# The expert block of a decoder layer: 14 whole tiles of 128 tokens in seven groups of two, instead of 16 batches of 112 tokens in four groups of four

## The chip, the core and the metric

The kernel runs on one core of a Trainium2 chip, in float32 for the part that matters here. The metric is the device time of one execution in microseconds (us). Matrix products run on TensorE (PE in the profile; PEld are its weight loads), the rest on VectorE (DVE), ScalarE (ACT) and GpSimd (POOL); SyncE (SP) issues all transfers.

## What is computed

A decoder of six sublayers over x of 16 batches x 112 tokens x 256 channels: causal linear attention, cross attention, an "ffn" block that holds a causal attention of its own and four experts, latent attention, windowed cross attention with rotary positions, and a ternary linear layer. The change touches the experts:

```python
xf = _rms(x, n2_w).reshape(-1, C)            # 1792 tokens x 256
logits = jnp.nan_to_num(xf @ gate_w.T)       # 1792 x 4
probs = jax.nn.softmax(logits, axis=-1)
topv, topi = jax.lax.top_k(probs, K)         # K = 2 of 4 experts
topv = topv / (topv.sum(-1, keepdims=True) + 1e-08)
wts = zeros(N, 4).at[arange(N)[:, None], topi].add(topv)
o0 = _gelu(xf @ e0_up.T) @ e0_down.T
o1 = jax.nn.silu(xf @ e1_w1.T) * (xf @ e1_w2.T) @ e1_down.T
o2 = _gelu(_gelu(_gelu(xf @ e2_l1.T) @ e2_l2.T) @ e2_l3.T) @ e2_l4.T
o3 = _gelu(_gelu(xf @ e3_down.T) @ e3_up.T) @ e3_out.T
moe = wts[:, 0:1] * o0 + wts[:, 1:2] * o1 + wts[:, 2:3] * o2 + wts[:, 3:4] * o3
moe = moe.reshape(B, T, C).at[:, :, :64].set(0.0)
return x + moe
```

All four experts are computed for every token; the weights `wts` choose afterwards. Hidden widths are 512 (256 for the first product of expert 3).

## The kernel before

Every engine has a program of its own, written out by hand, and the engines are tied by semaphores; there is no planner. Each engine executes its program in order. Nearly all matrix products go through one helper (`products`, whose line is L272), and nearly all transposes of rows through another (`transposes`, L265), so those two lines stand for many places of the code.

Tokens lie in rows: X holds 112 partitions (the tokens of a batch) x 16 x 256. The expert block has three parts.

**Preparation** (`phase_g`). For each of the 16 batches DVE scales 112 rows by their RMS factor (L1793), PE turns them into columns (L265), and ACT copies these into `m_xfT`, 128 channels x 2 x 1792 tokens, with the norm weight as scale (L1380). Four batches are prepared ahead of the first product; the other twelve are interleaved with the first twelve "up" products (`beside`).

**Gate.** Four products of gate weights (128x4) with 448 tokens each give logits as four rows of a bank; ACT copies them (L1395), 16 small transposes (L965) bring them back to tokens in rows, and DVE computes softmax, top 2 and weights in a chain of dependent steps (`weights`, L1810 to L1832), with one exponential on ACT (L1401).

**Experts** (`phase_m`). Four groups of `QUAD` = 4 batches, so `QN` = 448 token columns. The first group is written out, the other three are a loop. In a group PE makes 30 "up" products, each of 128 outputs x 448 tokens, contracted over 256 or 512 channels, so 2 or 4 matmuls of `QN` columns; in all 76 matmuls. In the profile each float32 matmul is two PE instructions, so 152. They rotate over four banks: product n may start when ACT has read product n-4. ACT reads them with GELU, Tanh or Copy (L1413 to L1419); DVE multiplies gate and up parts of expert 1 (L1842, L1845). The "down" products have tokens in rows as output: for each expert and batch a 112x192 result over 512 hidden channels (4 matmuls with 112 weight columns and 192 moving columns), 64 matmuls or 128 PE instructions in a group. DVE multiplies each with the token's weight and adds it to X (L1856).

After the last group all engines wait for the last of these additions (`M["acc"]`), and the latent attention starts on X, batch by batch, with layer norm statistics on DVE (L1764).

SP's queue is one program as well: in the causal attention before the experts it issues one small transfer of row maxima in each step (`maxima`, L470) and one expert weight after it (L371).

Of the kernel before, what the change touches and what calls it, by code (L numbers as in the profile page):

```python
# [28 lines left out]
ALU = mybir.AluOpType  # L29
# [26 lines left out]
UPS = 30  # L56

# [81 lines left out]
def decoder_kernel(nc, T, out):  # L139
    ctx = ExitStack()  # L140
    with ctx:
# [12 lines left out]
        X = sb("X", [S, B * D])  # L154
# [16 lines left out]
        def xb_(b, lo=0, hi=D):  # L171
            return X[:, bass.ds(b * D + lo, hi - lo)]

# [13 lines left out]
        gate = sb("gate", [P, KT, 4])  # L187
# [158 lines left out]
        m_xfT = take(P, KT * B * S, "p (k n) -> p k n", k=KT)  # L346
        g_xf = [take(S, D) for _ in range(2)]
        g_lt = take(4, B * S)
        g_lg = take(S, B * 4)
        g_a, g_b2, g_w = take(S, B * 4), take(S, B * 4), take(S, B * 4)  # L350
        g_red, g_red2 = take(S, B), take(S, B)
        g_cmp, g_cmp2 = take(S, B * 16), take(S, B * 16)
        m_g, m_s, m_u, m_t = (take(P, 2 * QN, "p (g n) -> p g n", g=2) for _ in range(4))
        m_h0, m_h1, m_ha, m_hb = (room[:, i * FT * QN:(i + 1) * FT * QN].rearrange("p (k n) -> p k n", k=FT) for i in range(4))
        m_hc = room[:, 4 * FT * QN:4 * FT * QN + KT * QN].rearrange("p (k n) -> p k n", k=KT)
        m_hd = take(P, FT * QN, "p (k n) -> p k n", k=FT)
# [20 lines left out]
        def _(sp):  # L377
            x_rows, x_out = T["x"].rearrange("b s d -> s b d"), X[:, :].rearrange("s (b d) -> s b d", b=B)
# [38 lines left out]
            wload(sp, gate[:, :, :], "gate", ld["gate"])  # L417
# [63 lines left out]
            sp.wait_ge(pre["pad"].sem, 3)  # L481
# [39 lines left out]
        def _(pe):  # L521
# [427 lines left out]
            def phase_g(b, u, half):  # L949
                pe.wait_ge(G["xf"].sem, G["xf"].at(b + 1))  # L950
                pe.wait_ge(G["xte"].sem, G["xte"].at(b - 1))
                transposes(g_xf[u], S, KT, pb[4 + u]).then_inc(G["xt"].sem, 1)

            def gate_of(i):
                pe.wait_ge(G["xte"].sem, G["xte"].at(QUAD * (i + 1)))
                if i > 1:
                    pe.wait_ge(G["ls"].sem, G["ls"].at(i - 1))
                products(pb[6 + i % 2][0:4, 0:QN], [gate[:, k, :] for k in range(KT)],
                         [m_xfT[:, k, i * QN:(i + 1) * QN] for k in range(KT)]).then_inc(G["lt"].sem, 1)

            def logits():
                pe.wait_ge(G["ls"].sem, G["ls"].at(B // QUAD))
                pe.wait_ge(G["xte"].sem, G["xte"].at(B))
                for b in range(B):
                    last = T3.transpose(pb[4][0:S, 4 * b:4 * b + 4], g_lt[:, b * S:(b + 1) * S], ident[0:4, 0:4])  # L965
# [14 lines left out]
            for b in range(QUAD):  # L980
                phase_g(b, b % 2, 0)


            def phase_m(i, first):
                use = [0]

                def up(w, m, src, kn, ready):
# [7 lines left out]
                    products(pb[n % 4][:, 0:QN], [w[:, k, m * P:(m + 1) * P] for k in range(kn)],  # L995
# [4 lines left out]
                def xf(k):  # L1000
                    return m_xfT[:, k, bass.ds(i * QN, QN)]
# [1002 lines left out]
```

## Time and profile before

| | |
|---|---|
| median of 3 runs | 1403.35 us (1402.88 to 1403.44) |
| profiled execution, its own time | 1402.48 us |
| span of its instructions | 1400.4 us |
| PE busy | 1333.6 us (95% of the span) |
| DVE, ACT, POOL busy | 738.0, 499.6, 286.4 us |
| mean granted TensorE clock | 0.987 of full speed |
| expert block, first up product to last addition | 750.07 to 1075.6 us |

Busy time of PE counts a matmul from its start to its modelled end; successive matmuls overlap in it. So the time that one matmul takes of a stream is read here as the distance from one start to the next: the start of one row of the timeline minus the start of the row before, divided by the instructions of the earlier row. Within one row, the last instruction starts at the row's end less the duration of one. An instruction's form is written as weight rows*weight columns, output shape, or as output<-input; `128*112 128x192` is a matmul with 112 weight columns and 192 moving columns.

### The profile page before, as it was taken

How to read it: one execution, taken by the hardware profiler on the slowest of the kernel's cores; microseconds unless marked ns; L12 is line 12 of the kernel's file. 1: busy time of each engine (PE TensorE's matmuls, PEld its weight loads, DVE VectorE, ACT ScalarE, POOL GpSimd, SP SyncE). 2: the span in 40 equal slices, each digit the busy share in tenths (PEclk: the TensorE clock that was granted, in tenths of full speed). 3: DMA queues.
4: the chain of work that ended last, by engine and by line, in shares of the span. 5: the costliest groups of instructions: out<-in, count | busy, mean ns of one | idle time of the engine just before them, and what ended most of it. 6: DMA issues, size and time to landing. Idle time of an engine off the chain costs nothing.

```text
span 1400.4 us, 30973 instructions
## 1 busy us (share of the span) xinstructions
PE 1333.6 (95%) x12381; PEld 922.9 (66%) x12381; DVE 738.0 (53%) x1715; ACT 499.6 (36%) x972; POOL 286.4 (20%) x380
## 2 busy tenths in 40 slices
PE   6999999988999999899988999999999899999996
PEld 5777888754666665467664575665757676777764
DVE  5666666654666664477743122020112555678886
ACT  2111111102555555356645223121221444444444
POOL 2000000102211221688724000000001100224431
PEclk9999999997999999999999999999999999999999
DMA  7212211102222220012200200000000000000001
GB/s 208 60 42 54 43 31 31 30 24 52 61 48 66 53 54 7 1 59 67 70 12 1 56 1 1 0 0 0 0 0 1 3 4 3 13 17 16 16 6 54
DMA packets 46995, 44.34 MB, mean 32 GB/s; under 512 B 14512, under 2 KB 43552, under 8 KB 46864
## 3 DMA queue, kind: packets, MB, share of 16 engines
q1 hardware_dynamic: 46864, 42.49, 11.9%
q8 instruction: 95, 1.56, 0.5%
q14 instruction: 36, 0.29, 0.1%
HBM read 38.95 MB, written 2.78 MB: 30 GB/s over the span
## 4 chain that ended last, share of the span: by engine, by line
PE 87%; ACT 4%; issue 3%; DVE 3%; POOL 2%; DMA 0%; ACTq 0%; DVEq 0%; POOLq 0%
PE banks L272 48%; PE banks L736 7%; PE banks L715 4%; PE banks L911 3%; PE banks L853 3%; PE banks L866 3%; PE banks L906 3%; PE banks L265 2%; PE banks L847 2%; PE banks L583 2%; PE banks L752 2%; ACT area L1280 2%; PE banks L541 2%; PE banks L894 2%; ACT area L1357 1%
## 5 line engine op out<-in xcount | busy, mean ns | idle before, releaser
L1620 DVE TENSOR_REDUCE Y_room<-banks 112x2 f32<-112x750 f32 x128 | 115.4, 936 | 85.9 <-PE banks L715 85.9
L1716 DVE TENSOR_REDUCE area<-banks 112x8 f32<-112x896 f32 x96 | 100.2, 1086 | 77.1 <-PE banks L853 77.1
L1280 ACT ACTIVATE area<-banks,Y_room 125x896 f32<-125x896 f32 x96 | 96.7, 1007 | 97.0 <-PE banks L736 87.1
L1357 ACT ACTIVATE area<-banks 112x896 f32<-112x896 f32 x96 | 82.8, 914 | 121.1 <-PE banks L911 121.1
L272 PE MATMUL banks<-room,area 128*112 128x256 f32 (+1 forms) x384 | 120.7, 465 | 3.8 <-issue 3.4
L1856 DVE SCALAR_TENSOR_TENSOR X<-banks,area,X 112x192 f32 (+1 forms) x64 | 26.5, 417 | 160.0 <-PE banks L272 160.0
L736 PE MATMUL banks<-room,area 64*125 64x224 f32 x768 | 100.0, 379 | 6.9 <-ACT area L1280 5.7
L272 PE MATMUL banks<-area,room 128*128 128x224 f32 x512 | 103.5, 362 | 2.0 <-ACT area L1233 2.0
L1413 ACT ACTIVATE room<-banks 128x448 f32<-128x448 f32 x72 | 39.2, 544 | 181.8 <-PE banks L272 181.8
L272 PEld LDWEIGHTS banks<-area,room 128*128 128x128 f32 x512 | 97.8, 194 | 4.6 <-ACT area L1233 2.3
L272 PE MATMUL banks<-room,l 128*128 128x448 f32 x256 | 97.9, 540 | 0.0
L251 POOL TENSOR_TENSOR rstd<-mv,kcol 112x1 f32<-112x1 f32 x32 | 6.1, 192 | 437.4 <-DVE mv L1455 437.4
L272 PEld LDWEIGHTS banks<-room,area 128*112 128x112 f32 x384 | 67.9, 182 | 41.1 <-issue 27.8
L736 PEld LDWEIGHTS banks<-room,area 64*125 64x125 f32 x768 | 65.7, 186 | 33.6 <-ACT area L1280 23.1
L1151 POOL TENSOR_TENSOR area<-area,kcol 112x32 f32<-112x32 f32 x16 | 87.2, 5451 | 1.3
L1222 ACT ACTIVATE area<-area,minus_one 128x448 f32<-128x448 f32 x64 | 42.8, 668 | 115.8 <-DVE area L1498 115.8
L265 PE MATMUL banks<-cst,area 112*128 112x112 f32 x416 | 65.5, 269 | 19.0 <-DVE area L260 10.7
L265 PEld LDWEIGHTS banks<-cst,area 112*128 112x128 f32 x416 | 46.8, 143 | 51.8 <-issue 45.1
L272 PEld LDWEIGHTS banks<-room,l 128*128 128x128 f32 x256 | 48.5, 190 | 47.6 <-issue 47.6
L1181 POOL MEMSET area<- 112x16 f32 x1 | 0.1, 125 | 318.5 <-DVE X L1856 318.5
L272 PEld LDWEIGHTS banks<-dn,room 128*112 128x112 f32 x384 | 62.6, 177 | 3.1 <-issue 3.1
L1498 DVE TENSOR_TENSOR area<-banks,bqk 128x448 f32<-128x448 f32 x64 | 39.9, 623 | 46.9 <-PE banks L272 39.8
(233 smaller groups left out, 2473.7 us busy)
## 6 DMA issues: line engine op xcount, KB each, us to landing
area<-den_scratch SPq DMA_DIRECT2D x32, 224.0 KB, 3.8
Y_room<-in_ctx SPq DMA_DIRECT2D x16, 375.0 KB
area<-in_ctxT SPq DMA_DIRECT2D x64, 93.8 KB
l<-in_l SPq DMA_DIRECT2D x2, 1024.0 KB, 5.2
room<-in_ctxT SPq DMA_DIRECT2D x16, 112.0 KB, 2.2
out<-X SPq DMA_DIRECT2D x16, 112.0 KB, 1.9
X<-in_x SPq DMA_DIRECT2D x1, 1568.0 KB, 21.9
room<-in_Wq SPq DMA_DIRECT2D x1, 1024.0 KB, 6.1
```

The lines of the kernel that those rows point to most:

```text
L265: last = nc.tensor.transpose(dst[:, k * parts:(k + 1) * parts], src[:, k * P:(k + 1) * P], ident[0:parts, 0:parts])
L272: last = nc.tensor.matmul(dst, a, w, start=(k == 0), stop=(k == len(lhs) - 1))
L715: last = T3.matmul(pb[r][0:S, 0:SC], b_q[w][o:o + HD + 2, k, r % 2, :], b_ctx[w][o:o + HD + 2, k, 0:SC], start=True, stop=True)
L736: last = T3.matmul(pb[4 + e][0:KC, 2 * i * S:2 * (i + 1) * S], b_ctx[w][o:o + 2 * SLOT, k, c * KC:(c + 1) * KC], b_q[w][o:o + 2 * SLOT, k, ...
L853: last = T3.matmul(pb[2 + j][0:S, c:c + S], c_qd[g % 3][o:o + SLOT, k, e, :], c_kT[g % 3][o:o + SLOT, k, :], start=False, stop=(k == 1 and ...
L866: last = T3.matmul(pb[6][SLOT * a:SLOT * a + HD + 1, t * S:(t + 1) * S], c_v[n % 2][:, 4 * t + a, :], c_pT[:, c:c + S], start=True, stop=True,
L1151: g_.tensor_tensor(c_r[n % 2], c_r[n % 2], kcol[:, 0, :], ALU.pow).then_inc(W["r"].sem, 1)
L1222: a_.activation(a_e[:, g % 2, :], a_z[:, g % 2, :], ACT.Exp, bias=minus_one[:, :]).then_inc(A["ex"].sem, 1)
L1280: a_.activation(b_pT[g][:, c, :, :], banks[0:KC, 4:6, 0:QN], ACT.Exp, bias=b_bias[v][:, c:c + 1]).then_inc(Bs["ex"].sem, 1)
L1357: a_.activation(c_pT[:, i * 8 * S:(i + 1) * 8 * S].rearrange("p (j n) -> p j n", j=2), banks[0:S, 2 + 2 * i:4 + 2 * i, 0:4 * S], ACT.Exp). ...
L1620: v_.tensor_reduce(b_nb[u][:, 4 * a + k:4 * a + k + H + 1:H], banks[0:S, 2 * a:2 * a + 2, 0:SC], AX_X, ALU.max, negate=True).then_inc(Bs[" ...
L1716: v_.tensor_reduce(c_nb[:, 8 * i:8 * i + 8].rearrange("q (j n) -> q j n", j=2), banks[0:S, 2 + 2 * i:4 + 2 * i, 0:4 * S].rearrange("q j (n ...
```

## The change

- X gets 128 partitions. The tokens of batches 0 to 13 stay where they are, in rows 0 to 111 of 14 tiles. Those of the last two batches are cut into seven pieces of 16 tokens each, and piece j fills rows 112 to 127 of tile j (batch 14) or 7+j (batch 15). 14 x 128 = 1792, so no row is empty.
- For the columns this is only a matter of where ACT writes: the columns of batch 14 and 15 go to seven places of 16 columns each. Batch 14 is prepared first (`XF_ORDER`), three batches ahead of the first product instead of four.
- `phase_m` takes two tiles (256 columns) at a time in seven groups; six of them are the loop.
- Down products have 128 weight columns (tokens) instead of 112; there are 2 per expert and group.
- The gate's weights are padded to 32 columns, and four blocks of up to 512 tokens are multiplied on four column groups of PE, in one bank; 4 transposes of up to 128x128 replace the 16 small ones. The weight chain on DVE runs on 128 partitions x 14 tiles instead of 112 x 16.
- Rows 112 to 127 of X collect only expert output: SP sets them to zero with 14 small transfers ahead of the first `maxima`. After group 3 seven transfers of 16 rows x 192 bring the pieces of batch 14 back into a 112-row tile beside the weights, after the last group seven more bring batch 15, issued in step 4 of the latent attention; DVE adds each of the two tiles to X before the statistics of batches 14 and 15.

```diff
+WHOLE = B - 2
+PIECE = P - S
+TILES = WHOLE
+PER = 2
+GN = PER * P
+GROUPS = TILES // PER
+ACCS = 4 * PER
+XF_ORDER = [WHOLE] + list(range(WHOLE // 2)) + [WHOLE + 1] + list(range(WHOLE // 2, WHOLE))
...
-        X = sb("X", [S, B * D])
+        X = sb("X", [P, B * D])
-        gate = sb("gate", [P, KT, 4])
+        gate = sb("gate", [P, KT, 32])
...
# SP, ahead of the first maxima
+            sp.wait_ge(pre["pad"].sem, 3)
+            for t in range(TILES):
+                sp.dma_start(X[S:P, t * D + FREE:(t + 1) * D], wuv[0:PIECE, 0:DO]).then_inc(ld["e0"].sem, 16)
...
+            def rests(i):
+                sp.wait_ge(M["acc"].sem, M["acc"].at(ACCS * ((WHOLE // 2 * (i + 1) + 1) // PER)))
+                for j in range(WHOLE // 2):
+                    t = WHOLE // 2 * i + j
+                    sp.dma_start(m_rest[i][PIECE * j:PIECE * (j + 1), :], X[S:P, t * D + FREE:(t + 1) * D]).then_inc(ld[("e0", "e3")[i]].sem, 16)
+            rests(0)
-            sp.wait_ge(M["acc"].sem, M["acc"].at(64))
+            sp.wait_ge(M["acc"].sem, M["acc"].at(ACCS * GROUPS))
             for n in range(B, 3 * B):
                 maxima(n)
+                if n == B + 4:
+                    rests(1)
...
# PE
+            def logits_of_columns():
+                pe.wait_ge(G["xte"].sem, G["xte"].at(B))
+                for k in range(KT):
+                    for i in range(4):
+                        n = min(QUAD, TILES - QUAD * i) * P
+                        last = T3.matmul(pb[6][32 * i:32 * i + 32, 0:n], gate[:, k, :],
+                                         m_xfT[:, k, QUAD * P * i:QUAD * P * i + n], start=(k == 0), stop=(k == KT - 1),
+                                         tile_position=(0, 32 * i))
+                last.then_inc(G["lt"].sem, 1)
...
-                if n < 12:
-                    phase_g(4 + n, n % 2, 0)
-                elif n < 16:
-                    gate_of(n - 12)
-                elif n == 18:
+                if n < B - 3:
+                    phase_g(3 + n)
+                elif n == 14:
+                    logits_of_columns()
+                elif n == 17:
                     logits()
...
-                    products(pb[n % 4][:, 0:QN], [w[:, k, m * P:(m + 1) * P] for k in range(kn)],
+                    products(pb[n % 4][:, 0:GN], [w[:, k, m * P:(m + 1) * P] for k in range(kn)],
...
-                    for j in range(QUAD):
-                        n = e * QUAD + j
+                    for j in range(PER):
+                        n = e * PER + j
                         if not first or n >= 4:
-                            pe.wait_ge(M["acc"].sem, M["acc"].at(16 * i + n - 3))
+                            pe.wait_ge(M["acc"].sem, M["acc"].at(ACCS * i + n - 3))
-                        products(pb[4 + j][0:S, 0:DO], [hsrc[:, k, j * S:(j + 1) * S] for k in range(FT)],
+                        products(pb[4 + n % 4][:, 0:DO], [hsrc[:, k, j * P:(j + 1) * P] for k in range(FT)],
...
# DVE, statistics of the latent attention
+                        if B + WHOLE <= n < 2 * B:
+                            i = n - B - WHOLE
+                            dve.wait_ge(ld[("e0", "e3")[i]].sem, 16 * ((2 + TILES, 3)[i] + WHOLE // 2))
+                            v_.tensor_tensor(xb_(n - B, FREE), xb_(n - B, FREE), m_rest[i], ALU.add).then_inc(pre["kn"].sem, 1)
+                            dve.wait_ge(pre["kn"].sem, i + 2)
                         v_.bn_stats(stats[:, :], xb_(n % B)).then_inc(W["chain"].sem, 1)
```

## Rows read from the trace of the kernel before

**Rows 1.** The page: the chain that ended last, shares of the span by engine.
```profile
PE 87%; ACT 4%; issue 3%; DVE 3%; POOL 2%; DMA 0%; ACTq 0%; DVEq 0%; POOLq 0%
```

**Rows 2.** The chain, 740 to 1085 us: start, length, engine, count.
```profile
745.82 3.01 DVE area L1793 x4
...
750.07 3.18 PE banks L272 x4
...
796.20 278.84 PE banks L272 x1032
```

**Rows 3.** One loop group: stretch, length, busy PE, PEld, DVE, ACT, POOL; clock.
```profile
841.09:919.01 77.92, 77.92 (x281) 49.65 (x281) 13.41 (x32) 18.06 (x34) 0.00 (x0) 1.00 0.00 1
```

**Rows 4.** Timeline of PE in the first group of the loop.
```profile
865.14 12.19 PE L272 MATMUL banks<-room,l 128*128 128x448 f32 x32
877.17 5.36 PE L272 MATMUL banks<-dn,room 128*112 128x192 f32 x32
882.37 3.17 PE L272 MATMUL banks<-area,d 128*128 x8
```

**Rows 5.** Timeline of PE in the linear attention: other widths and forms.
```profile
44.05 6.32 PE L272 MATMUL banks<-area,room 128*128 128x224 f32 x32
50.21 3.62 PE L272 MATMUL banks<-room,area 128*112 128x256 f32 x16
53.76 0.97 PE L535 MATMUL banks<-area 112*32 112x112 f32 x32
```

**Rows 6.** Timeline of PE in the latent attention: 128 weight columns, 112 moving.
```profile
1109.97 1.15 PE L804 MATMUL banks<-area,wuqk 128*128 128x112 f32 x8
```

**Rows 7.** Groups by line: busy us, mean ns of one, idle before.
```profile
L272 PE MATMUL banks<-Y_room,room 128*112 128x256 f32 x128 | 33.0, 380 | 0.0
...
L804 PE MATMUL banks<-area,wuqk 128*128 128x112 f32 x128 | 19.1, 294 | 0.0
...
L535 PE MATMUL banks<-area 112*32 112x112 f32 x512 | 15.6, 262 | 1.2 <-DVE area L1489 1.2
...
L272 PEld LDWEIGHTS banks<-room,l 128*128 128x128 f32 x256 | 48.5, 190 | 47.6 <-issue 47.6
```

**Rows 8.** Timeline of PE in the first group of the experts.
```profile
753.28 1.68 PE L272 MATMUL banks<-area,up 128*128 128x448 f32 x4
...
754.99 1.68 PE L272 MATMUL banks<-area,up 128*128 128x448 f32 x4
...
770.88 0.41 PE L265 MATMUL banks<-cst,area 112*128 112x112 f32 x2 [0.50 <-DVE area L1793]
...
774.46 1.67 PE L272 MATMUL banks<-area,gate 128*4 128x448 f32 x4
...
785.95 9.29 PE L272 MATMUL banks<-room,l 128*128 128x448 f32 x24
795.16 1.03 PE L965 MATMUL banks<-cst,area 4*112 4x4 f32 x16
```

**Rows 9.** Timeline of ACT in the first group.
```profile
766.99 0.54 ACT L1416 ACTIVATE area<-banks 128x448 f32<-128x448 f32 x1 [0.68 <-PE banks L272]
767.43 0.54 ACT L1417 ACTIVATE area<-banks 128x448 f32<-128x448 f32 x1
767.85 0.60 ACT L1380 ACTIVATE area<-banks,n 128x112 f32<-128x112 f32 x2
```

**Rows 10.** The three microseconds after the first up product starts: stretch.
```profile
750.00:753.00 3.00, 2.93 (x4) 1.40 (x5) 0.28 (x1) 1.22 (x1) 3.00 (x6) 0.51 0.00 0
```

**Rows 11.** Waits of SP's queue, 480 to 745 us: total, times, longest.
```profile
SPq L470 <- ACT area L1362: 162.7, 16, 43.2
```

**Rows 12.** Timeline of SP's issues in the latent attention, 1085 to 1240 us.
```profile
1090.93 106.30 SPq L470 DMA_DIRECT2D room<-area  x13
1197.28 0.43 SPq L506 DMA_DIRECT2D room<-in_ctxT  x1
```

**Rows 13.** Waits, 1090 to 1220 us: total, times, longest.
```profile
DVE area L1716 <- PE banks L853: 45.3, 15, 3.4
```

More of the change, by code:

```diff
@@ L345, in decoder_kernel @@
         top[0] = 0
-        m_xfT = take(P, KT * B * S, "p (k n) -> p k n", k=KT)
+        m_xfT = take(P, KT * TILES * P, "p (k n) -> p k n", k=KT)
         g_xf = [take(S, D) for _ in range(2)]
[L348 to L356, printed above, removed]
+        g_lt = take(P, QUAD * P)
+        g_lg = take(P, TILES * 4)
+        g_a, g_b2, g_w = take(P, TILES * 4), take(P, TILES * 4), take(P, TILES * 4)
+        g_red, g_red2 = take(P, TILES), take(P, TILES)
+        g_cmp, g_cmp2 = take(P, TILES * 16), take(P, TILES * 16)
+        m_g, m_s, m_u, m_t = (take(P, 2 * GN, "p (g n) -> p g n", g=2) for _ in range(4))
+        m_h0, m_h1, m_ha, m_hb = (room[:, i * FT * GN:(i + 1) * FT * GN].rearrange("p (k n) -> p k n", k=FT) for i in range(4))
+        m_hc = room[:, 4 * FT * GN:4 * FT * GN + KT * GN].rearrange("p (k n) -> p k n", k=KT)
+        m_hd = take(P, FT * GN, "p (k n) -> p k n", k=FT)
+        m_rest = [Y_room[0:S, (B - 2) * D + i * DO:(B - 2) * D + (i + 1) * DO] for i in range(2)]
         f_xn = room[0:S, 1024:1024 + B * D]
@@ L946, in _, with phase_g @@
             attention(0, B, -2, B + 3)
[L949 to L959, printed above, removed]
+            def phase_g(i):
+                pe.wait_ge(G["xf"].sem, G["xf"].at(i + 1))
+                pe.wait_ge(G["xte"].sem, G["xte"].at(i - 1))
+                transposes(g_xf[i % 2], S, KT, pb[4 + i % 2]).then_inc(G["xt"].sem, 1)
@@ L961, in logits @@
             def logits():
-                pe.wait_ge(G["ls"].sem, G["ls"].at(B // QUAD))
+                pe.wait_ge(G["ls"].sem, G["ls"].at(1))
                 pe.wait_ge(G["xte"].sem, G["xte"].at(B))
-                for b in range(B):
-                    last = T3.transpose(pb[4][0:S, 4 * b:4 * b + 4], g_lt[:, b * S:(b + 1) * S], ident[0:4, 0:4])
+                for j in range(QUAD):
+                    n = P if QUAD * 3 + j < TILES else 96
+                    last = T3.transpose(pb[4][:, j * P:j * P + n], g_lt[0:n, j * P:(j + 1) * P], ident[0:n, 0:n])
@@ L979, in _ @@
             pe.wait_ge(ld["gate"].sem, 16)
-            for b in range(QUAD):
-                phase_g(b, b % 2, 0)
+            for i in range(3):
+                phase_g(i)
             def phase_m(i, first):
@@ L1074, in _ @@
             g_.memset(wuqk[:, :, :], 0.0).then_inc(pre["pad"].sem, 1)
+            g_.memset(gate[:, :, :], 0.0).then_inc(pre["scale"].sem, 1)
             pool.wait_ge(pre["pad"].sem, 2)
@@ L1375, in _, with phase_g @@
             attention(0, B, -2, B + 4)
-            def phase_g(b, u, half):
-                act.wait_ge(G["xt"].sem, G["xt"].at(b + 1))
+            def phase_g(i):
+                b = XF_ORDER[i]
+                act.wait_ge(G["xt"].sem, G["xt"].at(i + 1))
                 for k in range(KT):
-                    last = a_.activation(m_xfT[:, k, bass.ds(b * S, S)], pb[4 + u][:, k * S:(k + 1) * S], ACT.Copy,
-                                         scale=n12[:, 2 + k:3 + k])
+                    src = pb[4 + i % 2][:, k * S:(k + 1) * S]
+                    if b < WHOLE:
+                        dst = m_xfT[:, k, b * P:b * P + S]
+                    else:
+                        half = slice((b - WHOLE) * WHOLE // 2 * P, (b - WHOLE + 1) * WHOLE // 2 * P)
+                        dst = m_xfT[:, k, half].rearrange("p (t n) -> p t n", n=P)[:, :, S:P]
+                        src = src.rearrange("p (t n) -> p t n", n=PIECE)
+                    last = a_.activation(dst, src, ACT.Copy, scale=n12[:, 2 + k:3 + k])
@@ L1788, in _, with phase_g @@
             attention(0, B, -2, B + 3, None)
-            def phase_g(b, u, half):
-                dve.wait_ge(G["xt"].sem, G["xt"].at(b - 1))
-                v_.tensor_scalar(g_xf[u], yb_(b), rms[:, bass.ds(B + b, 1)], None, ALU.mult).then_inc(G["xf"].sem, 1)
+            def phase_g(i):
+                b = XF_ORDER[i]
+                dve.wait_ge(G["xt"].sem, G["xt"].at(i - 1))
+                v_.tensor_scalar(g_xf[i % 2], yb_(b), rms[:, B + b:B + b + 1], None, ALU.mult).then_inc(G["xf"].sem, 1)
             dve.wait_ge(G["pc"].sem, G["pc"].at(3))
-            for b in range(B - FT):
-                phase_g(b, b % 2, 0)
+            for i in range(B - FT):
+                phase_g(i)
             steps = [0]
```

85 lines of the change are left out of this document (44 added, 41 removed).

## The prediction, as put on record before the changed kernel ran

> **What bounds the kernel now.** I read the page first: TensorE is busy 95% of the span (the table above) and holds 87% of the chain that ended last [rows 1]. So only a change in what TensorE does, or in what it waits for, can move the time. Then the chain in the stretch of the expert block: from 796.20 us on, one piece of 278.84 us and 1032 recorded instructions of L272 with nothing between [rows 2]. In the loop of `phase_m` TensorE is the only bound. The window of one whole group confirms it: 77.92 us, PE busy all of it, ACT 18.06, DVE 13.41 [rows 3].
>
> So I need the spacing of matmuls in a stream. The timeline gives 32 instructions of 448 columns in 877.17 - 865.14 = 12.03 us, 0.376 us each, and 32 of 192 columns in 882.37 - 877.17 = 5.20 us, 0.1625 us each [rows 4]. Check: 152 x 0.3758 + 128 x 0.1625 = 57.1 + 20.8 = 77.9 us, the whole group. Therefore nothing else is paid in a group: not the turn of the loop, not a semaphore wait, not a weight load.
>
> **The steady groups.** The up products keep their columns: 4 x 448 = 7 x 256 = 1792. What changes is only the number of instructions, 4 x 152 = 608 before and 7 x 152 = 1064 after. The price of one of 256 columns by interpolation between the two widths: 0.1625 + 64 x (0.3758 - 0.1625) / 256 = 0.2158 us. The trace has such a width elsewhere: 16 instructions in 3.62 us, the last starting 0.38 us before the end, so 3.24 / 15 = 0.216 us [rows 5, 7]. They agree. Up products: 608 x 0.3758 = 228.5 us before, 1064 x 0.2158 = 229.6 after: +1.1 us.
>
> The down products lose instructions: 4 x 128 = 512 before, 7 x 4 experts x 2 tiles x 4 x 2 = 448 after, with the same 192 moving columns. The weights are 128 columns wide instead of 112. Does that cost? With 128 weight columns and only 112 moving ones the spacing is (1.15 - 0.29) / 7 = 0.123 us, with 0.29 the duration of one [rows 6, 7]; so a load of 128 columns fits under anything longer than that, and 0.1625 is longer. I take 0.1625: 83.2 us before, 72.8 after, -10.4 us. Per group the new cost is 152 x 0.2158 + 64 x 0.1625 = 43.2 us; 7 groups 302.4 against 4 x 77.92 = 311.7: **-9.3 us**. The upper bound on both comes from the row that is nearest in both weight width and moving width, 128 x 224: (50.21 - 44.05) / 32 = 0.1925 us [rows 5], 3 ns above the interpolated 0.1892. If wide weights really cost 3 ns, it is 1064 x 0.003 + 448 x 0.003 = +4.5 us. I take the interpolation, because the 448-wide stream has 128-wide weights too and shows nothing of it; that 224-wide row holds waits between its blocks.
>
> A rule speaks against the change. The Trainium skill, "TensorE: Matmul & The Clock Gate", section "The mechanism", says that a weight load overlaps running matmuls only if its row group differs; all loads here use all rows, so by it each instruction would pay its load. By that rule the trace would differ, and it disagrees: a load is recorded with 0.19 us [rows 7], and the spacing of 0.1625 us for 192 columns is less than the load alone [rows 4].
>
> **ACT and DVE under the shorter products.** An up product of two matmuls lasts 0.86 us instead of 1.50. ACT starts its reads 0.44 us apart at 448 columns (766.99 to 767.43) with a duration of 0.54 [rows 9]; at 256 columns it lies between 0.25 (in proportion) and 0.44; I take 0.28. The heaviest pair, gate and up, needs three reads, 0.84 us for 1.73 us of TensorE; at 0.44 they would take 1.32, so cover remains at either end. The waits of down products and of `l2`, `l3`, `up3` on ACT each have at least two products of other kinds between, 1.7 us or more. DVE is busy 13.41 of 77.92 us and keeps the same elements [rows 3]. The loop's turn comes six times instead of three, at the cost of nothing so far [rows 3].
>
> **The gate.** Before, the stretch with four gate products and three up products between runs from 774.46 to 785.95 us, 11.49 us [rows 8]; less 3 x 1.50 us, the gate costs 7.0 us. After: 16 instructions, in fours on four column groups. The trace has this form, 32 weight columns at four column positions: 32 instructions of 112 columns in 0.97 us, (0.97 - 0.26) / 31 = 0.023 us each [rows 5, 7], a quarter of what 112 columns take. So four rounds of 512 columns at 0.43 us (0.3758 + 64 x 0.000833) are 1.7 us, with a seam 1.8: **-5.2 us**. If the column groups did not overlap: 12 x 0.43 + 4 x 0.216 = 6.0 us, -1.0. The 16 small transposes take about 1.0 us [rows 8], the four big ones 4 x 0.12 = 0.5, at the spacing of [rows 6]: **-0.5 us**.
>
> **The first group's other edits.** A pair of transposes between up products costs (754.99 - 753.28) - 1.50 = 0.21 us [rows 8]; 13 instead of 12 stand inside: +0.2. One batch fewer comes ahead of the first up product. The chain there goes over DVE's row scaling, four batches in 3.01 us, 0.75 each [rows 2]: -0.7. TensorE waited 0.50 us for DVE's row scaling behind the products of expert 1 [rows 8]; the new group has one more up product between them, the DVE operations there are 256 wide, and the wait goes: -0.5. Against it stands the clock: from 750 to 753 us it is granted at 0.51, so 1.2 GHz, after the preparation, in which TensorE waited for each batch [rows 10]; the first product takes 3.18 us [rows 2] for 1.5. I assume that half speed ends at the same time as before, so beginning 0.7 us earlier adds some 0.3. In the interleaved part a step of TensorE takes 4 x 0.216 + 0.21 = 1.07 us, ACT's step 0.28 + 0.60 = 0.88, with a gate part 1.16 [rows 9]; the mean of the two is 1.02, just covered. I take nothing for it, up to +3 us if not. The weight chain has 2.6 + 1.7 + 6.9 + 3.5 + 2.6 = 17.3 us of products to hide in (down of expert 0, `d3`, `l3`, `up3`, down of expert 1) before the fifth down product needs its first addition.
>
> **What is added elsewhere.** SP waits 43.2 us in a row for the first `maxima`, the longest of its waits there [rows 11]; 14 issues at 0.43 us [rows 12] to twice that, 6 to 12 us, fit in: nothing. In the latent attention `maxima` comes 13 times in 106 us, every 8.9 us [rows 12], and seven issues at 0.43 to 0.86 us end before the next: nothing. If TensorE had to wait for all of them, it would be 6 us, once. The two additions of 112x192 on DVE (like operations of DVE follow each other at 0.75 us in [rows 2], waits and all) stand in steps where DVE waits up to 3.4 us for TensorE [rows 13]: nothing; without that cover, 1.5 us. The memset of the gate's padding is in the first microseconds of POOL.
>
> **Sum.** -9.3 - 5.2 - 0.5 + 0.2 - 0.7 - 0.5 + 0.3 = -15.7 us. The profiled execution took 1402.48 us, 2.1 more than its span; 1402.48 - 15.7 = 1386.8. The median of the runs lies 0.87 above that execution, so **1387.7 us**.
>
> **Rivals.**
> - *The column groups do not overlap* with all 128 rows in use (the row that I read uses 112), or they do and the seam is long. For: the exact form is not in the trace. Against: the quarter is exact for its neighbour. +4.3: 1392 us.
> - *Wide weights cost their 3 ns*, as the 224-wide row could be read: +4.5, 1392 us.
> - *The first group becomes bound by ACT or DVE*: 13 steps with 0.05 us of room on average. +1 to +4, 1389 to 1392 us. A waits row of PE on L1380 or L1793 would show it.
> - *Slower: weight loads are no longer hidden.* The block has 392 more instructions (1512 against 1120). The duration of a load is 0.19 us for 128 columns. If the shorter stream left each exposed, it is +74 us less 15.7: about 1461; it decides from 0.04 us per added instruction on. For: load and product of a 256-column instruction are nearly equal in recorded duration (0.19 against 0.216) [rows 7]. Against: with 192 columns nothing shows [rows 4]. The Trainium skill, on the same page under "LDWEIGHTS (loading the stationary operand)", gives 107 ns for 128 columns; by that, called an estimate, it would be +42 and 1430 us.
> - *No change*: several covers fail together, or the spacing of the down products becomes the load's 0.19 us (448 x 0.0275 = +12.3 us, 1400 us).
>
> **Chances.** The forecast 0.62, with a range of its own of 1385 to 1390.5 (a half-speed window more or less after the block's end, which may fall otherwise on shifted work, is worth 1.7 us). Gate 0.11, wide weights 0.12, first group 0.08, slower 0.04, no change 0.03. Within 0.2% is what a measurement of this kernel cannot tell from none. Faster 0.93, same 0.03, slower 0.04. The range from 1384.5 to 1393.5 takes in the three middle rivals.
>
> **What the profile would show.** Windows of a loop group at 43.2 us with PE busy throughout; starts 0.216 us apart at 256 columns and 0.1625 at 192 with 128-wide weights; the gate in one row of 16 within 1.9 us; the first up product near 749.3 us and the last addition near 1060; `maxima` steps of the latent attention still 8.9 us apart, also around the new transfers. The prediction fails if groups take more than 45 us, if PE's waits on ACT or DVE appear within the loop, or if the step in which SP issues seven transfers is longer than its neighbours.

## The result, and the profile after

The changed kernel takes 1384.79 us in the median of 4 runs (1383.37 to 1386.48); the kernel before, beside it on the same chip, took 1403.12 (1402.37 to 1403.44). The ratio is 0.9872, with a 95% interval of 0.9858 to 0.9885: 18.3 us, or 16.1 to 19.9, are gone. 15.7 were forecast, as 1387.7 us; the forecast's own range was 1385 to 1390.5, so 1384.79 lies 0.2 us below it, inside only the wider range from 1384.5.

The profiled execution took 1383.37 us, its span is 1381.6. It is the fastest of the four, 1.4 us below their median. The page of the changed kernel, busy times and then the shares of the chain (compare [rows 1]):

```profile
PE 1315.9 (95%) x12761; PEld 997.1 (72%) x12761; DVE 738.9 (53%) x1733; ACT 514.1 (37%) x1073; POOL 286.5 (21%) x381
...
PE 87%; ACT 3%; issue 3%; DVE 3%; POOL 2%; DMA 0%; SPq 0%; ACTq 0%; DVEq 0%; POOLq 0%
```

TensorE is the bound as before; PE's busy time fell by 17.7 us. The shares alone say nothing about where. For that, the chain through the block, as [rows 2]: start, length, what.

```profile
744.16 2.29 DVE area L1836 x3
...
747.69 2.04 PE banks L280 x4
...
772.00 285.22 PE banks L280 x1432
...
1057.36 0.43 DVE X L1900
```

The last addition in the chain of before:

```profile
1075.18 0.43 DVE X L1856
```

From the first up product to the last addition the block takes 1057.36 - 747.69 = 309.67 us. Before, it was 1075.18 - 750.07 = 325.11: **-15.44 us**. The preparation in front, from the first row scaling to the first up product, takes 747.69 - 744.16 = 3.53 us instead of 750.07 - 745.82 = 4.25 [rows 2]: **-0.72**. Together -16.2. The span shrank by 18.8, so 2.6 us lie outside the block: 1.66 ahead of it (the first row scaling starts at 744.16 instead of 745.82) and 1.0 behind it (324.2 us from the last addition to the end, 325.2 before). These 2.6 us need a cause of their own.

Most of the 1.66 us is there before the kernel is 30 us old. The timeline of PE where the first 64 products of 224 columns end, and the window around it; first before, then after:

```profile
28.65 1.04 PE L583 MATMUL banks<-area 64*112 64x112 f32 x16
...
15.00:30.00 15.00, 15.00 (x79) 14.10 (x78) 8.73 (x15) 5.26 (x8) 0.00 (x0) 1.00 0.91 211
```

```profile
27.58 1.04 PE L606 MATMUL banks<-area 64*112 64x112 f32 x16
...
15.00:30.00 15.00, 15.00 (x81) 13.64 (x81) 9.67 (x17) 5.34 (x8) 0.00 (x0) 1.00 0.77 199
```

TensorE is 28.65 - 27.58 = 1.07 us ahead there, at a granted clock of 1.00 (the number behind the last count) in both, while the first transfers are under way (the large transfer of x took 21.9 us from issue to landing before and 17.0 after). In the other profiles of the changed kernel's program the same row starts at 27.26 us (e0), 28.23 (e1) and 27.14 (e5), with that of before at 28.43 (e2) and 28.29 (e4). What makes it vary is not shown.

Inside, the window of one loop group (as [rows 3]) and the timeline of PE in it (as [rows 4]):

```profile
797.81:841.02 43.21, 43.21 (x219) 39.28 (x218) 8.47 (x24) 12.62 (x34) 0.00 (x0) 1.00 0.00 1
```

```profile
811.62 7.07 PE L280 MATMUL banks<-room,l 128*128 128x256 f32 x32
818.53 2.76 PE L280 MATMUL banks<-dn,room 128*128 128x192 f32 x16
821.13 1.89 PE L280 MATMUL banks<-area,d 128*128 x8
```

A group is 43.21 us (43.2 forecast), with PE busy all of it. 32 instructions of 256 columns take 818.53 - 811.62 = 6.91 us, 0.2159 each (0.2158 interpolated); 16 of 192 columns, now with 128 weight columns, 2.60 us, 0.1625 each, as with 112. No row of PE waits for anything between 797 and 1057 us. The second number in the window is new: weight loads are recorded for 39.28 of 43.21 us, where they were 49.65 of 77.92 [rows 3], and still they cost nothing.

The first group, timeline of PE (as [rows 8]):

```profile
765.19 1.92 PE L982 MATMUL banks<-area,gate 128*32 128x512 f32 x16
767.03 1.13 PE L280 MATMUL banks<-area,u 128*128 128x256 f32 x4
...
771.46 0.55 PE L992 MATMUL banks<-cst,area 128*128 128x128 f32 x4
771.84 3.64 PE L280 MATMUL banks<-room,l 128*128 128x256 f32 x16
```

The gate takes 767.03 - 765.19 = 1.84 us, the four transposes 0.38. No row of PE has a wait in brackets from the first up product on: the stall on VectorE [rows 8] is gone. It was worth more than its bracket of 0.50 us. Timeline of PE before:

```profile
768.70 1.68 PE L272 MATMUL banks<-area,g 128*128 128x448 f32 x4
...
771.13 1.68 PE L272 MATMUL banks<-area,u 128*128 128x448 f32 x4
```

From one up product to the next are 2.43 us, where the steps without a wait take 1.71 (754.99 - 753.28): 0.72.

The transfers, timeline of SP; and the step of the latent attention read from PE's products with `wuqk`, around the seven transfers of `rests(1)`:

```profile
549.29 9.24 SPq L479 DMA_DIRECT2D X<-wuv  x14
592.47 0.83 SPq L484 DMA_DIRECT2D room<-area  x1
...
928.19 4.38 SPq L517 DMA_DIRECT2D Y_room<-X  x7
...
1107.35 5.19 SPq L517 DMA_DIRECT2D Y_room<-X  x7
```

```profile
1100.00 1.15 PE L827 MATMUL banks<-area,wuqk 128*128 128x112 f32 x8
...
1108.89 1.15 PE L827 MATMUL banks<-area,wuqk 128*128 128x112 f32 x8
...
1117.78 1.15 PE L827 MATMUL banks<-area,wuqk 128*128 128x112 f32 x8
```

14 issues take 9.24 us and end 34 us before the first `maxima` is due; seven take 5.19 us in a step of 8.89 us, and the step stays 8.89.

### The profile page after: what moved, and what is told of

Its sections match the earlier page's. It is cut to its first block, busy times and chain, and to the rows that moved or that the text cites. A ratio compares the mean times of both kernels' runs of the same rounds, so it can differ in the third digit from the quotient of the medians.

```text
span 1381.6 us, 32117 instructions
## 1 busy us (share of the span) xinstructions
PE 1315.9 (95%) x12761; PEld 997.1 (72%) x12761; DVE 738.9 (53%) x1733; ACT 514.1 (37%) x1073; POOL 286.5 (21%) x381
## 4 chain that ended last, share of the span: by engine, by line
PE 87%; ACT 3%; issue 3%; DVE 3%; POOL 2%; DMA 0%; SPq 0%; ACTq 0%; DVEq 0%; POOLq 0%
PE banks L280 47%; PE banks L759 7%; PE banks L738 4%; PE banks L934 3%; PE banks L876 3%; PE banks L889 3%; PE banks L929 3%; PE banks L273 2%; PE banks L870 2%; PE banks L606 2%; PE banks L775 2%; PE banks L564 2%; ACT area L1308 2%; PE banks L917 2%; ACT area L1385 1%
## 5 line engine op out<-in xcount | busy, mean ns | idle before, releaser
L1450 ACT ACTIVATE room<-banks 128x256 f32<-128x256 f32 x126 | 48.4, 384 | 170.1 <-PE banks L280 170.1
L1900 DVE SCALAR_TENSOR_TENSOR X<-banks,area,X 128x192 f32 (+1 forms) x56 | 23.3, 418 | 165.0 <-PE banks L280 165.0
L280 PE MATMUL banks<-room,l 128*128 128x256 f32 x448 | 99.2, 379 | 0.0
L280 PEld LDWEIGHTS banks<-room,l 128*128 128x128 f32 x448 | 85.0, 190 | 11.5
L738 PE MATMUL banks<-area,room 18*112 18x375 f32 x512 | 63.1, 537 | 0.6 <-DVE Y_room L1657 0.6
```

What stands on the lines that cost most here:

```text
L280: last = nc.tensor.matmul(dst, a, w, start=(k == 0), stop=(k == len(lhs) - 1))
L738: last = T3.matmul(pb[r][0:S, 0:SC], b_q[w][o:o + HD + 2, k, r % 2, :], b_ctx[w][o:o + HD + 2, k, 0:SC], start=True, stop=True)
L1450: a_.activation(dst[:, m, :], src, ACT.Gelu).then_inc(M["ev"].sem, 1)
```

## The experiments

Two theories compete for the size. *The mechanism of the prediction*: 15.7 us in the block, and what is beyond it falls out of where the stretches of half TensorE speed lie, which differs between executions. *Another source*: a part of the change that was priced at nothing or too low (gate, wide products, transfers) brings the rest. The kernel before took 1402.67 us (15 runs) beside e0, e1, e2 and e4, 1402.54 (9 runs) beside e3, e5, e6 and e7, and 1401.96 (7 runs) beside e8; ratios are to these.

### e0: the changed kernel again

No edit.

> The changed kernel once more, unchanged, to see how much one execution differs from the next. Theory A (half-speed stretches of TensorE account for what lies beyond the forecast): the executions fall into two clusters some 3 us apart, near 1383.4 and 1386.3 us, and the upper cluster has the lower mean granted clock (0.986 against 0.988); the median lands between 1383 and 1387. Rival B (the extra gain over the forecast is in the expert block): all executions keep the same mean clock and the spread has no relation to it.

1384.25 us (1382.40 to 1386.10, 4 runs), ratio 0.9863 (0.9848 to 0.9878). Its profile fell on the slowest of the four, 1386.10 us, which makes it useful: the same kernel, 2.7 us longer than in the profile above. The chain:

```profile
748.53 2.29 DVE area L1836 x3
...
1060.08 0.43 DVE X L1900
```

The timeline of PE, first up product:

```profile
752.06 1.10 PE L280 MATMUL banks<-area,up 128*128 128x256 f32 x4 [0.78 <-ACT area L1416]
```

The block is *shorter* here, 1060.08 - 752.06 = 308.02 us instead of 309.67, because the first products run at full speed (1.10 us for four, where the chain above has 2.04). But the preparation began 4.4 us later (748.53 to 744.16). So ahead of the block the same kernel varies by more than the 1.66 us that were to be explained.

The windows from 280 to 370 us show most of what varies; the granted clock is the number behind the last count. First the kernel before, then the changed kernel, then its repetition:

```profile
280.00:370.00 90.00, 81.34 (x749) 48.80 (x748) 49.80 (x92) 24.06 (x33) 13.02 (x21) 0.89 0.19 44
```

```profile
280.00:370.00 90.00, 81.83 (x779) 49.48 (x779) 50.88 (x94) 24.17 (x33) 13.39 (x21) 0.89 0.20 44
```

```profile
280.00:370.00 90.00, 81.64 (x729) 48.62 (x729) 48.38 (x90) 22.58 (x32) 11.88 (x20) 0.85 0.20 44
```

A mean clock of 0.85 instead of 0.89 over 90 us is 0.04 x 90 = 3.6 us of work at full speed that did not get done, in the same program. Another half-speed stretch lies at 733 to 737 us in e0 (granted clock 0.57), ahead of the block and not in it. The kernel before and the changed one, however, have the same 0.89 here: their 1.66 us do not come from this stage.

The expectation spoke of two clusters near 1383.4 and 1386.3 us. The eight executions are spread more evenly (1382.40, three at 1383.4, 1385.12, three from 1386.10 to 1386.48), but the order of their clocks is exactly that of their times: 0.989, 0.988, 0.987, 0.986. The product of span and mean granted clock is nearly the same for all eight, 1364.9 to 1365.4 us, though the spans differ by 4.1. So Theory A holds in this, and Rival B (no relation to the clock) does not. For the 31 executions of the kernel before that stand beside the experiments this product is 1381.4 us in the mean (1379.3 to 1382.6), 16.2 above the 1365.1 of the changed kernel. That is an estimate, since the clocks are given to 0.001, or 1.4 us of a span; it is the size of what the trace gives for the block and its preparation. The rest goes with the mean clock, 0.9873 for 0.9863.

### e1: the gate's loops the other way round

```diff
-                for k in range(KT):
-                    for i in range(4):
+                for i in range(4):
+                    for k in range(KT):
```

> The changed kernel with the two loops of the gate product swapped: the column group is the outer loop, the contraction the inner one. The 16 instructions are the same. Theory A (the four column groups overlap, but only instructions that follow each other in different groups): within a group the four instructions follow at 0.43 us, the next group starts under the last of them, so the block takes (4 + 3 + 3 + 3) x 0.43 less the short fourth group, about 5.0 us instead of 1.8, and the kernel is 3 to 3.5 us slower, 1388 us. Rival B (the overlap does not depend on the order): no change, 1384.8 us. Both leave the rest of the block alone.

Timeline of PE:

```profile
766.07 1.93 PE L982 MATMUL banks<-area,gate 128*32 128x512 f32 x16
767.93 1.13 PE L280 MATMUL banks<-area,u 128*128 128x256 f32 x4
```

1.86 us instead of 1.84, and 1383.94 us in all (1383.64 to 1387.18), ratio 0.9872 (0.9857 to 0.9887). Theory A, about 5.0 us for the row, is refuted: the order does not matter. Windows on the gate's line show how the row begins, first in the changed kernel, then here:

```profile
765.00:765.30 0.30, 0.11 (x4) 0.11 (x8) 1.00 0.93 266
```

```profile
766.00:766.20 0.20, 0.13 (x4) 0.13 (x8) 1.00 0.98 348
```

Four matmuls have started within 0.13 us in both. In e1 the first four of the program all belong to one column group, and four of 512 columns one after another take 4 x 0.43 = 1.7 us, nearly the whole row. So the trace is read like this: each column group works through its own four, and a group need not wait for the instructions of another group that stand ahead of its own.

### e4: the kernel before with the new gate alone

```diff
+            def logits_of_columns():
+                for k in range(KT):
+                    for i in range(4):
+                        last = T3.matmul(pb[6][32 * i:32 * i + 32, 0:QN], gate[:, k, :],
+                                         m_xfT[:, k, QN * i:QN * i + QN], start=(k == 0), stop=(k == KT - 1),
+                                         tile_position=(0, 32 * i))
```

and four transposes of 128x112 in place of the 16 small ones.

> The kernel before with the gate of the change alone: padded weights, four column groups of 448 tokens, four transposes. Nothing else is changed. Theory A (the parts of the change add up): 7.0 + 1.0 us become 1.5 + 0.1 + 0.4, so 5.5 to 6 us less than before, 1397.5 us. Rival B (the gate was partly hidden, or its gain belongs to the rest): less than 3 us of gain, 1400 us or more.

1396.11 us (1395.58 to 1399.03), ratio 0.9956 (0.9943 to 0.9970): -6.6 us, interval 4.2 to 8.0. Timeline of PE:

```profile
776.70 1.71 PE L959 MATMUL banks<-area,gate 128*32 128x448 f32 x16
778.34 1.77 PE L272 MATMUL banks<-area,u 128*128 128x448 f32 x4
...
785.96 0.60 PE L967 MATMUL banks<-cst,area 128*112 128x128 f32 x4
786.39 6.18 PE L272 MATMUL banks<-room,l 128*128 128x448 f32 x16
```

1.64 + 0.43 = 2.07 us for what was 7.0 + 1.0: -5.9, and the block, 749.21 to 1068.35, is 319.14 us, -5.97 against before. This third of the gain has nothing to do with the tiles. All four blocks are 448 wide here, so the row also gives the speed of four column groups: in series it would be 16 x 0.3758 = 6.01 us, and 6.01 / 1.64 = 3.7 times.

### e2: the kernel before in eight groups of two batches

```diff
+PER = 2
+GN = PER * S
+GROUPS = B // PER
-            with pe.Fori(1, B // QUAD) as i:
+            with pe.Fori(1, GROUPS) as i:
```

224 columns at a time, no full tiles, the old gate.

> The kernel before with eight groups of two batches (224 columns) instead of four of four (448); tokens, gate and tiles as before. Theory A (only streamed columns count, with 2.4 ns per instruction): up products 8 x 152 x 0.1892 = 230.1 us against 228.5, down products unchanged, so +1.6 us in the block, less 0.5 to 1.5 us because the first group's interleaved part waits less for DVE: 1403 us, plus or minus 1.5. Rival B (smaller groups are a gain of their own, by shorter waits between stages): clearly faster than before, 1398 us or less. Rival C (weight loads begin to show at 224 columns, 0.1925 us as in the linear attention's row): 1216 x 0.003 = +3.7 us more, 1407 us.

1403.75 us (1401.14 to 1406.32, 11 runs), ratio 1.0007 (0.9997 to 1.0016). Timeline of PE in the second group:

```profile
814.24 6.22 PE L276 MATMUL banks<-room,l 128*128 128x224 f32 x32
820.29 2.76 PE L276 MATMUL banks<-dn,room 128*112 128x192 f32 x16
```

(820.29 - 814.24) / 32 = 0.1891 us. The interpolation said 0.1892; the 0.1925 that I had read in the linear attention [rows 5] belongs to that stage, not to the width. So the forecast's rival *wide weights cost 3 ns* rested on a reading that includes something else. And the size of the group brings nothing by itself: 8 x 152 x 0.1891 = 230.0 us for 228.5, and Rival B (1398 us or less) is out.

### e3: 14 groups of one tile

```diff
-PER = 2
+PER = 1
```

on the changed kernel: up products of 128 columns, 2128 + 448 instructions.

> The changed kernel with fourteen groups of one tile (128 columns) instead of seven of two. 14 x 152 = 2128 instructions of 128 columns for the up products, the down products unchanged at 448. Theory A (only streamed columns count): spacing 0.109 us, 232 us against 229.6, the kernel at 1387 to 1390 us with the first group's losses. Rival B (a load of 128 weight columns takes about 0.12 us of its own and shows as soon as the product is shorter): spacing 0.12 to 0.123 us, 255 to 262 us, the kernel at 1410 to 1420 us, and PEld busy without a gap. Rival C (ACT bounds the gate and up products: three reads in two products of 0.49 us): on top of either, 4 pairs x 14 groups x up to 0.2 us = 11 us, seen as waits of PE on ACT.

1394.79 us (1392.95 to 1395.83), ratio 0.9938 (0.9925 to 0.9952): 10.0 us above the 1384.79 of the changed kernel. The total lies between Theory A (1387 to 1390) and Rival B (1410 to 1420). Window of one group, and the timeline of PE in it:

```profile
779.84:802.01 22.17, 22.17 (x186) 22.17 (x185) 5.73 (x20) 8.69 (x34) 0.00 (x0) 1.00 0.00 1
```

```profile
786.98 3.74 PE L280 MATMUL banks<-room,l 128*128 128x128 f32 x32
790.55 1.47 PE L280 MATMUL banks<-dn,room 128*128 128x192 f32 x8
```

PE is busy all of the window, so it waits for ScalarE nowhere in it (Rival C is out). Weight loads are recorded as busy all 22.17 us too, and the stream still runs at 3.57 / 32 = 0.1116 us for 128 columns. The block has 14 x 184 = 2576 such instructions, 1064 more than the changed kernel; had each of these exposed a load of 0.19 us [rows 7], the time would have risen by 202 us. The groups are 14 x 22.17 = 310.4 us against 302.5, +7.9: 2128 x 0.1116 = 237.5 for 1064 x 0.2159 = 229.7. Part of it is the fixed share of an instruction: the spacings at 192, 224, 256 and 448 columns (0.1625, 0.1891, 0.2159, 0.3758 us) lie on a line of 0.833 ns a column and 2.5 ns. By it 128 columns would be 0.1092 us; the measured 0.1116 is 2.4 ns more, 5.1 us of the 7.9. That the loads are these 2.4 ns is likely, not shown: they fill the window. The block is 318.1 us (750.30 to 1068.40) for 309.67, so the first group adds 0.5; the other 1.6 of the 10.0 us lie outside the block. The product of span and clock as in e0 is 1372.4 us, 7.2 above the changed kernel's, and the mean clock is lower (0.9858 for 0.9873), so the clock can account for them.

### e5: no return of the pieces

```diff
-            rests(0)
-                if n == B + 4:
-                    rests(1)
-                            v_.tensor_tensor(xb_(n - B, FREE), xb_(n - B, FREE), m_rest[i], ALU.add).then_inc(pre["kn"].sem, 1)
```

> The changed kernel without the fourteen transfers that bring the pieces back and without DVE's two additions; the output of batches 14 and 15 lacks the experts' part. Theory A (all of it is hidden): no difference, 1384.8 plus or minus 1.5 us, and the steps of the latent attention stay 8.9 us apart. Rival B (the seven issues on SP or the additions on DVE delay a step): 1 to 6 us faster.

Batches 14 and 15 lack the experts' part. 1384.54 us (1382.36 to 1386.68), ratio 0.9876 (0.9861 to 0.9891); block 1056.36 - 746.66 = 309.70 us. With the return the block was 309.67, and the medians differ by 0.3 us where the interval is some 2 us to either side: no cost of the fourteen transfers and two additions can be seen.

### e6 and e8: groups of four tiles

Three groups of 512 columns and one of 256, so five batches are prepared ahead of the first product; two buffers of hidden values lie elsewhere, everything else is as in the changed kernel.

```diff
-PER = 2
+PER = 4
-                if n < B - 3:
-                    phase_g(3 + n)
+                if n < B - 5:
+                    phase_g(5 + n)
+            phase_m(GROUPS, False, TAIL)
```

> The changed kernel with whole tiles but in three groups of four (512 columns) and one of two (256), five batches prepared ahead of the first product instead of three; two of the hidden buffers lie elsewhere. Theory A (the gain is in the whole tiles and the gate, not in the group size): up products 456 x 0.4291 + 152 x 0.2158 = 228.5 us against 229.6, two more batches ahead of the first product +1.5 us: 1385.2 us, within 2 us of the changed kernel. Rival B (groups of two are what brings the gain, through shorter stages): 5 us or more slower, 1390 us and up.

1390.16 us (1388.21 to 1392.78), ratio 0.9907 (0.9890 to 0.9923): some 5 us above Theory A (1385.2 us) and just where Rival B had it, for which groups of two are the gain. Its profile fell on the slowest of the four, 1392.78. Timelines of PE and of VectorE in the first group:

```profile
771.56 1.89 PE L282 MATMUL banks<-area,u 128*128 128x512 f32 x4
775.86 0.41 PE L275 MATMUL banks<-cst,area 112*128 112x112 f32 x2 [2.40 <-DVE area L1842]
776.11 3.18 PE L282 MATMUL banks<-area,g 128*128 128x512 f32 x4
```

```profile
774.13 0.69 DVE L1892 SCALAR_TENSOR_TENSOR area<-area 128x512 f32<-128x512 f32 x1 [5.86 <-ACT area L1461]
774.85 0.69 DVE L1895 SCALAR_TENSOR_TENSOR room<-area 128x512 f32<-128x512 f32 x1
775.46 0.61 DVE L1842 TENSOR_SCALAR area<-Y_room,rms 112x256 f32<-112x256 f32 x2
```

The transposes are ahead of the products by two batches more, but VectorE's program was left as it was: the scaling of batch 12 stands behind the first pair of expert 1, which waits for ScalarE to read a product that TensorE has just made. TensorE waits 2.40 us, and the four instructions after it take 3.18 us recorded for 1.89, at half speed. e8 changes only that:

```diff
-            for i in range(B - FT):
+            for i in range(B):
                 phase_g(i)
-                    if first and m < 2:
-                        for n in range(2):
-                            phase_g(B - FT + 2 * m + n)
```

> This is the kernel of groups of four tiles with one thing changed: VectorE scales the rows of all 16 batches before it turns to the first pair of expert 1, where before the last four scalings stood between its pairs. Theory A (what four tiles lost was this order alone): TensorE's wait of 2.40 us on the scaling at 775.9 us goes, and with it the half-speed stretch behind it, in which a step took 3.18 + 0.58 us recorded for 1.89 + 0.36, so 1.5 us; together 3.9 us: 1386.3 us, the interleaved steps all 1.93 us apart, the first group 93 us from first up product to the next group's. What is left above the changed kernel, some 2 us, is two more batches ahead of the first product (1.5 us), less 532 x 0.0024 = 1.3 us of fewer instructions, plus noise. Rival B (512-wide products or the larger groups cost something elsewhere, and the wait only stood in a place where there was slack): no change, 1389 to 1391 us, with no wait but the same end. Rival C (the half-speed stretches only move to another place, as they did when TensorE was kept busy ahead of the block): half of it, 1388 us.

1385.65 us (1385.00 to 1386.25), ratio 0.9882 (0.9865 to 0.9898); 1386.3 was Theory A. (The 532 fewer instructions in its sum are 1064 - 608 = 456, so 1.1 us instead of 1.3.) The interleaved steps are 1.93 us apart without a gap; timeline of PE:

```profile
769.28 1.89 PE L282 MATMUL banks<-area,u 128*128 128x512 f32 x4
771.02 0.36 PE L275 MATMUL banks<-cst,area 112*128 112x112 f32 x2
771.21 1.90 PE L282 MATMUL banks<-area,g 128*128 128x512 f32 x4
```

The first group fell from 96.88 to 93.41 us and the block from 312.35 to 308.89, -3.46. From the product at 769.28 to the gate are 10.83 us instead of 15.14, so the wait and the half speed behind it were worth 4.3; 0.8 of that went to a longer half-speed stretch at the block's start (the first two steps take 6.45 us for 5.61). So the order of one engine's program was the loss, not the width, and Rivals B and C are out. From the start of the preparation to the last addition it is 1058.24 - 744.14 = 314.1 us, where the changed kernel has 313.2; with the 0.9 between them and the medians 0.9 apart, groups of two or of four tiles cannot be told apart.

### e7: TensorE kept busy until the first product

```diff
-            keep_busy(3, 24)
+            keep_busy(3, 29)
             for i in range(3):
                 phase_g(i)
+                keep_busy(3, (1, 1, 4)[i])
```

> The changed kernel with TensorE kept busy by spare products ahead of the block: 29 instead of 24 before the first batch, and 1, 1 and 4 after the first three. Nothing computed is changed. Theory A (the half-speed stretch of 3.4 us at the block's start comes from TensorE's waits during preparation, and costs 1.7 us): the granted clock stays full there and the kernel gains 1 to 1.7 us, 1383.3 us, if the spare products don't delay the batches. Rival B (the clock falls there whatever TensorE does): no gain, and up to 1 us lost to the spare products.

1385.42 us (1385.09 to 1385.87), ratio 0.9877 (0.9862 to 0.9892). Timeline of PE:

```profile
748.55 0.92 PE L654 MATMUL banks<-masks_b,ident_b 112*112 112x448 bf16 x4
749.50 1.10 PE L280 MATMUL banks<-area,up 128*128 128x256 f32 x4
```

and the window behind the block, where the changed kernel is granted 1.00:

```profile
1057.00:1085.00 28.00, 23.31 (x239) 16.78 (x238) 14.18 (x43) 9.72 (x26) 8.49 (x17) 0.88 0.01 2
```

The first products run at 2.4 GHz, and the block is 1057.52 - 749.50 = 308.02 us, 1.65 less. It is not in the total. In this execution a half-speed stretch came behind the block, 326.6 us from the last addition to the end instead of 324.2. One profile doesn't show that the first caused the second.

## Why the prediction was right, and where it was short

**The groups, the largest term.** Forecast -9.3; measured 7 x 43.21 = 302.5 for 311.7: -9.2. Both prices held within 0.1 ns, and e2 confirmed the interpolation at a third width. The rule of the Trainium skill ("TensorE: Matmul & The Clock Gate", section "The mechanism") that spoke against the change is contradicted more strongly than before: full-row loads follow full-row products at 0.1625 us with 128 weight columns, and at 0.1116 in e3, with 0.19 us recorded for the load. The slower rival (1461 us) is out. Its threshold was 0.04 us for each added instruction; in e3 the groups grew by 7.9 us for 1064 added ones, 7 ns each.

**Gate and logits.** Forecast -5.2 and -0.5; measured 7.0 to 1.84 and 1.0 to 0.38 us, -5.2 and -0.6, and e4 has the two alone at -5.9. The rival without overlap of the column groups (6.0 us) is refuted by the row of 16. In e4, with four equal blocks, the gain is 3.7 times, 0.92 of the number of groups. The Trainium skill has a neighbour on the same page: "Measured speedup vs the span model" gives three column tiles 2.38 times, 0.79 of their number. The trace does not agree with that share, it is higher here.

**The first group's other edits.** Stall -0.5: gone, and mis-sized, since the forecast took the bracket for the cost: -0.72. One pair of transposes more, +0.2: the steps are 1.07 us as computed, with no wait, so the rival *bound by ACT or DVE* did not occur. One batch fewer ahead, -0.7: measured -0.72. Clock, +0.3: the first two steps take 2.21 and 1.65 us for 1.07 each, 1.7 us lost, where before lost 1.5: +0.2. That this fits the forecast is luck. It assumed that half speed ends at the same time as before; but from 751.5 to 752.5 us the granted clock was 0.50 before and is 1.00 now, and the first up product came 2.4 us earlier, not 0.7. With the old end, 2.4 us earlier at half the speed would have been +1.2. The terms give -16.0, the trace -16.2.

**What was taken for nothing** shows no cost: zeroing (9.24 us, within the 6 to 12 allowed), returns and additions (e5), the loop's turns (no gap in the stream).

**What the prediction was short of** is 2.6 us of the spans, against 0.5 in the block and its preparation. So the mechanism held, but that the total lies inside the stated range is in part luck: 1384.79 is 0.3 us above its lower end, 1384.5, and the repetition e0, at 1384.25, would lie outside. It allowed 1.7 us for a half-speed window "more or less after the block's end". There it was worth 1.0. One more row of before, behind the block, windows of the trace:

```profile
1080.00:1084.00 4.00, 3.46 (x17) 3.11 (x16) 1.98 (x9) 0.98 (x3) 1.49 (x4) 0.58 0.00 0
```

Another 1.66 us lie *ahead* of the block, in work that the change leaves as it was, and the prediction did not allow for any. They are not the clock's: 1.07 of them arise in the first 28 us at full clock, and the granted clock from 280 to 370 us is the same before and after. The other 0.6 us have no row.

In four profiles with the changed kernel's program ahead of and behind the block (it, e0, e1, e5) the first up product starts at 747.69, 752.06, 748.54 and 746.66 us, mean 748.7; in three with that of before (it, e4, e2) at 750.07, 749.21, 749.70, mean 749.7. The difference is 0.9, and 0.7 of it is the batch. The spread of 5.4 us within one program is larger than anything outside the block that was to be explained. So these profiles do not show that the 1.66 us are a property of the change, and e0 shows that they need not be. The 1.0 us behind the block is less clear: the four changed ones have 324.1 to 324.2 us there, the three others 325.2, 325.9 and 324.2, e3 325.2, e6 326.2, and e7 and e8 326.6 and 325.3.

The medians' difference is 18.3 and 18.4 us, with intervals that begin at 16.1 and 17.1. Of it, 16.2 are the block and its preparation, by the trace, and by the product of span and clock over 8 and 31 executions. The other 2 us go with a mean granted clock that is 0.001 higher. That is as much as the clock differs from one execution to the next, but in a mean of 8 against 31 executions it may well belong to the change. No run shows whether it does, or how.

## What to carry to other kernels

When TensorE's stream has no gaps, price a new tiling by the number of instructions times the start-to-start distance at their width, and read that distance from a stream of long blocks in the same stage: 0.1892 us for 224 columns was right and 0.1925 from a stage with seams was not. Filling the tile in the dimension that is paid per instruction (tokens among the weight columns of the down products: 448 instead of 512) is what gains in the stream; group size made no clear difference between 224 and 512 columns and cost 10 us at 128. The cost of a wait is the step with it less the step without it (0.72 us), not its bracket (0.50). If one engine's work is pulled ahead, move the same step ahead in the program of every engine that feeds it, and price changes of 1 to 3 us against several executions, since the time of work that was not touched moves that much. If the granted clock of each execution is known, compare span times clock as well: here it cuts a spread of 4.1 us to 0.5.

## What the runs showed of the chip that I had not expected

- **Order of column groups.** 16 float32 instructions of up to 512 columns on four column groups take 1.84 us with the groups alternating and 1.86 with all instructions of one group together (e1); in both, four of them have started within 0.13 us, also where the first four of the program belong to one column group.
- **Where the line ends.** Spacings of float32 instructions in a full-speed stream with 128 weight columns: 0.1116 us at 128 columns, 0.1625 at 192, 0.1891 at 224, 0.2159 at 256, 0.3758 at 448. From 192 up they lie on one line; at 128, with the loads recorded as busy without a gap, 2.4 ns come on top. A load's recorded duration of 0.19 us is therefore no price.
- **The clock in executions of one kernel.** Eight executions of the changed kernel took 1382.4 to 1386.5 us. Span times mean granted clock is 1364.9 to 1365.4 us for all of them. The two profiled ones differ by 2.7 us in time and by 0.89 to 0.85 in granted clock between 280 and 370 us; a block that starts at full speed is 1.65 us shorter (308.02 to 309.67, in e0 and in e7 alike) and did not make the whole shorter in either.
